# A DLRM tower: ten tables looked up by matmul instead of nine, two late tables for three chunks instead of two, and the whole order of the later stages rewritten

## The reference

```python
e = jnp.stack([tbl_0[ids[:, 0]], ..., tbl_26[ids[:, 26]]], axis=1)      # (512, 27, 128)
interactions = jnp.einsum('bfd,bgd->bfg', e, e)
x = interactions.reshape(B, F * F)[:, TRIL_IDX]                          # 351 pairs, i > j
h = jnp.concatenate([bottom, x, bottom], axis=1)                         # (512, 607)
h = jnp.maximum(h @ W_top1 + b_top1, 0.0)                                # 512 wide
h = jnp.maximum(h @ W_top2 + b_top2, 0.0)                                # 256 wide
y = h @ W_top3
```

## Time and profile before

| | |
|---|---|
| median of 3 runs | 121.84 us (120.61 to 122.99) |
| the profiled execution's own time | 119.64 us |
| its span | 117.5 us |
| busy: PE, DVE, ACT, POOL | 92.8, 74.8, 63.7, 72.8 us |
| gathers | 68, of 1.05 us on average |
| mean DMA rate | 121 GB/s |

### The profile page before, as it was taken

How to read it: one execution, slowest core, us unless ns; L and a number is a source line. 1 busy time by engine, 2 the same in 40 slices (tenths; PEclk the granted TensorE clock), 3 DMA queues, 4 the chain that set the end, 5 groups by cost and what they waited for, 6 DMA issues and landing times.

```text
span 117.5 us, 3583 instructions
## 1 busy us (share of the span) xinstructions
PE 92.8 (79%) x1464; PEld 77.8 (66%) x1464; DVE 74.8 (64%) x230; ACT 63.7 (54%) x150; POOL 72.8 (62%) x75
## 2 busy tenths in 40 slices
PE   6608999999899999794458399955899838992992
PEld 6503788878688788583357299843798718980990
DVE  5418899999999999864994062164154656793001
ACT  7525698997996985563162162361165506990010
POOL 2777777777777787777777777677677620001000
PEclk9999999999999999999999967999999999999689
DMA  3749999999999767793112212113122220000000
GB/s 39 164 132 261 252 248 237 242 244 247 230 242 234 179 165 214 290 300 92 46 45 76 62 50 67 50 50 86 49 59 59 58 58 6 0 6 21 0 0 1
DMA packets 7347, 14.28 MB, mean 121 GB/s; under 512 B 2149, under 2 KB 4485, under 8 KB 7332
## 3 DMA queue, kind: packets, MB, share of 16 engines
q1 hardware_dynamic: 5104, 9.58, 32.8%
q0 software_dynamic: 2208, 4.47, 14.5%
q10 hardware_dynamic: 20, 0.01, 0.1%
HBM read 13.81 MB, written 0.00 MB: 118 GB/s over the span
## 4 chain that ended last, share of the span: by engine, by line
POOL 59%; issue 18%; PE 10%; DMA 6%; DVE 3%; ACTq 1%; DVEq 0%
POOL rows L309 59%; PE pH L587 5%; DMA rows<-in_tbl,ids_sb 3%; DVE Z L342 3%; PE pT L587 2%; PE pG L613 2%; DMA ids_sb<-in_ids 2%; DMA Z<-Z 1%; PE pF L538 1%; ACTq L247 1%; PE pT L527 1%; DVE prod L484 0%; DVE ET L321 0%; DVEq L129 0%
## 5 line engine op out<-in xcount | busy, mean ns | idle before, releaser
L309 POOL DMA_INDIRECT rows<-in_tbl,ids_sb x68 | 71.6, 1054 | 21.6 <-issue 20.4
L465 DVE TENSOR_SCALAR hot<-ids_b,row_f 125x512 fp32r<-125x512 int16 (+1 forms) x75 | 31.8, 452 | 1.7 <-DMA ids_b<-in_ids_t 1.7
L342 DVE COPY Z<-pG 26x96 f32<-26x96 f32 (+1 forms) x80 | 19.5, 244 | 19.5 <-PE pG L613 18.5
L342 ACT COPY Z<-pG 26x96 f32<-26x96 f32 (+1 forms) x80 | 18.7, 234 | 16.3 <-PE pG L613 15.4
L563 PE MATMUL pG<-hot,high 125*128 125x512 f32 x72 | 22.0, 422 | 4.7 <-ACT high L352 4.2
L563 PE MATMUL pG<-hot,low 125*128 125x512 f32 x72 | 20.2, 404 | 0.0
L462 DVE TENSOR_TENSOR low<-tbl,high 125x256 fp32r<-125x256 f32 x44 | 18.2, 414 | 3.1 <-ACT high L352 3.1
L563 PEld LDWEIGHTS pG<-hot,high 125*128 125x128 f32 x72 | 13.6, 196 | 9.3 <-ACT high L352 4.5
L613 PE MATMUL pG<-ET 128*26 128x26 f32 x1024 | 13.5, 194 | 7.1 <-issue 4.6
L613 PEld LDWEIGHTS pG<-ET 128*26 128x26 f32 x1024 | 11.2, 104 | 10.1 <-issue 7.9
L563 PEld LDWEIGHTS pG<-hot,low 125*128 125x128 f32 x72 | 14.1, 196 | 3.1
(11 more groups left out here) (39 smaller groups left out, 57.6 us busy)
## 6 DMA issues: line engine op xcount, KB each, us to landing
tbl<-in_tbl SPq DMA_DIRECT2D x11, 448.0 KB
ids_b<-in_ids_t SPq DMA_DIRECT2D x9, 128.0 KB, 5.2
rows<-in_tbl,ids_sb POOLq DMA_INDIRECT x68, 5.0
W1Z<-in_w_tiles SPq DMA_DIRECT2D x1, 768.0 KB
tbl<-in_tbl SPq DMA_DIRECT2D x11, 52.0 KB
W1A_B<-in_w_ab SPq DMA_DIRECT2D x1, 512.0 KB, 3.8
W2S<-in_W_top SPq DMA_DIRECT2D x1, 512.0 KB
botT<-in_bottom_t SPq DMA_DIRECT2D x1, 256.0 KB, 4.0
```

The lines of the kernel that those rows point to most:

```text
L309: pool.indirect_dma_start(out=rows[:, c % 2, slot[f], :], out_offset=None, in_=tables[f][:, :], in_offset=bass.IndirectOffsetOnAxis(ap=ids ...
L342: last = engine_copy(to[:, :, STAGE - n:STAGE, :, s, :], of)
L465: nc.vector.tensor_scalar(hot[0:TP, n % 2, k, columns(n)], ids_b[0:TP, n % TABLE_RING, columns(n)], row_f[0:TP, k:k + 1], None, ALU.is_equ ...
```

## The change

- `N_ONE_HOT` 9 to 10: one more table is looked up for all samples. `LATE_FROM` 2 to 1: the two late tables are looked up for samples 128 to 511, 384 columns instead of 256. All twelve 1000-row tables are now looked up. Gathers: 17 + 15 + 15 + 15 = 62. Chunks 1 and 2 have seven runs instead of six, the last chunk eight instead of seven.
- In `look_up` PE takes all 8 blocks of `high`, then all 8 of `low`; DVE makes all its `hot` blocks and then the four `low` parts, where they alternated.
- The first table is loaded and rounded in two halves, and the second table's loads no longer wait for the first ids. SP's loads of weights don't wait for the last table or for `W1A_B`. ACT copies the previous lookup before it makes one-hot blocks.
- 72 warm-up matmuls instead of 34.
- DVE prepares **both** late tables ahead of the first Z move; before, the second came after the first unit of chunk 0.
- Both gram units of a chunk stand back to back. The first dense layer of a chunk follows the next chunk's grams, and in the last step chunk 2's first and second layers also stand ahead of chunk 3's last transposes; chunk 3's four gram units stand together.

```diff
-N_ONE_HOT = 9
+N_ONE_HOT = 10
-LATE_FROM = 2
-WARM_UP = (20, 14)
+LATE_FROM = 1
+WARM_UP = 72
...
-                elif n:
-                    sp.wait_ge(ids_b_in[n - 1], 16)
...
-            sp.wait_ge(tbl_in[N_ALL - 1], 32)
...
-            sp.wait_ge(w1ab_in, 16)
...
             prepare(N_ONE_HOT)
+            prepare(N_ONE_HOT + 1)
             for c in range(LAST):
-                first, *others = units_of(c)
-                move_gram(nc.vector.tensor_copy, dve, first, 0, z_dve)
-                runs_of(c + 1, 0, BETWEEN[c])
+                for k in units_of(c):
+                    move_gram(nc.vector.tensor_copy, dve, k, 0, z_dve)
+                runs_of(c + 1, 0, 2)
                 if c == 0:
-                    prepare(N_ONE_HOT + 1)
                     dve.wait_ge(w1ab_in, 16)
                     nc.vector.tensor_tensor(W1AB[:, :], W1A_B[:, 0, :], W1A_B[:, 1, :], ALU.add).then_inc(w1ab_done, 1)
-                for k in others:
-                    move_gram(nc.vector.tensor_copy, dve, k, 0, z_dve)
-                runs_of(c + 1, BETWEEN[c], RUNS[c + 1] - LATE_RUNS[c + 1])
+                runs_of(c + 1, 2, 4)
                 if c:
                     dense3(c - 1)
-                runs_of(c + 1, RUNS[c + 1] - LATE_RUNS[c + 1], RUNS[c + 1])
+                if c + 1 == LAST:
+                    dense3(c)
+                runs_of(c + 1, 4, RUNS[c + 1])
...
+                for k in units_of(c):
+                    gram_unit(k)
+                next_run()
+                next_run()
                 if c == 0:
                     look_up(N_ONE_HOT)
+                    next_run()
+                    look_up(N_ONE_HOT + 1)
+                    next_run()
+                    dense_layer1_bottom(c)
                 else:
+                    dense_layer1_pairs(c - 1)
+                    next_run()
+                    dense_layer2(c - 1)
+                if c + 1 < LAST:
+                    while len(waiting):
+                        next_run()
+                    if c:
+                        dense_layer1_bottom(c)
+                else:
                     dense_layer1_bottom(c)
+                    dense_layer1_pairs(c)
+                    next_run()
+                    dense_layer2(c)
+                    while len(waiting):
+                        next_run()
```

More of the change, by code:

```diff
@@ L200, in dlrm_tower_kernel @@
         z_dve = sem("z_dve")
-        packed = sem("packed")
+        packed = [sem(f"packed_{c}") for c in range(CHUNKS)]
         packed_pool = sem("packed_pool")
@@ L532, in dense_layer2 @@
                     pe.wait_ge(lookup_moved, N_ALL)
+                    pe.wait_ge(weights_in, 3 * 16)
                 if 0 < c < LAST:
@@ L543, in _ @@
             pe.wait_ge(warm_done, 1)
-            for x in range(sum(WARM_UP)):
+            for x in range(WARM_UP):
                 nc.tensor.matmul(pF[:, 0:P], warm[:, :], warm[:, :], start=True, stop=True)
@@ L550, in look_up @@
                     pe.wait_ge(lookup_moved, n)
-                half = TABLE_K // 2
-                first, second = range(half), range(half, TABLE_K)
-                for x, (part, blocks) in enumerate(((high, first), (low, first), (high, second), (low, second))):
-                    if x == 0:
-                        pe.wait_ge(high_done, n + 1)
-                    for k in blocks:
+                for part in (high, low):
+                    for k in range(TABLE_K):
+                        if part is high and k % (TABLE_K // 2) == 0:
+                            pe.wait_ge(high_done, n + 1 + (n > 0 or k > 0))
                         if part is high and k < TABLE_K - act_blocks[n]:
@@ L564, in look_up @@
                                                 hot[0:TP, n % 2, k, columns(n)],
-                                                start=x == 0 and k == 0, stop=x == 3 and k == TABLE_K - 1)
+                                                start=part is high and k == 0, stop=part is low and k == TABLE_K - 1)
                 last.then_inc(looked_up, 1)
@@ L633, in _, with next_run @@
                     pe.wait_ge(mover(i), moved_until(c, i))
-                waiting = list(range(RUNS[c + 1] - LATE_RUNS[c + 1]))
-                def next_run(until):
-                    if waiting and waiting[0] < until:
-                        transpose_run(c + 1, waiting.pop(0))
-                first, *others = units_of(c)
-                gram_unit(first)
-                next_run(BETWEEN[c])
+                waiting = list(range(RUNS[c + 1]))
+                def next_run():
+                    transpose_run(c + 1, waiting.pop(0))
@@ L657, in _ @@
-                while waiting and waiting[0] < BETWEEN[c]:
-                    next_run(BETWEEN[c])
-                for k in others:
-                    gram_unit(k)
-                next_run(len(RUNS) * P)
-                if c == 0:
-                    dense_layer1_bottom(c)
-                    look_up(N_ONE_HOT + 1)
-                next_run(len(RUNS) * P)
-                if c:
-                    dense_layer2(c - 1)
-                if c + 1 == LAST:
-                    dense_layer1_bottom(c)
@@ L687, in _ @@
             pe.wait_ge(h2_done, LAST)
-            nc.tensor.matmul(pF[:, :], ones[0:1, :], b2_sb[0:1, :], start=True, stop=False)
+            nc.tensor.matmul(pF[:, 0:N2], ones[0:1, :], b2_sb[0:1, :], start=True, stop=False)
             wait_packed(LAST)
```

105 lines of the change are left out of this document (45 added, 60 removed).

## The result

| | before | after |
|---|---|---|
| median | 121.22 us (120.29 to 122.99) | 131.67 us (129.8 to 131.97) |
| profiled execution, its span | 119.64, 117.5 us | 131.37, 129.6 us |
| gathers: number, mean, last one starts | 68, 1.05 us, 93.92 | 62, 1.28 us, 99.92 |

The change makes the kernel slower: ratio 1.080, 95% interval 1.057 to 1.103. Medians are of all executions; a ratio with an interval compares only the undisturbed ones of both kernels. The forecast was 123.4 us with a range up to 126.8, most likely a difference too small to tell, so it was wrong.

What follows compares the result with a forecast made beforehand. The prediction took POOL's gathers to bound the kernel before, then summed DVE's and PE's serial steps to 116.9 us, plus 1.4 for a stop and 0.8 for low clock: span 119.1, time 123.4 us, range 120.4 to 126.8.

Steps and rivals of the forecast that it cites:

- What the change removes: Six gathers on POOL: the last starts at 86.4 instead of 93.9 us, worth 7.5 us if gathers stayed the bound.
- The front: Work up to DVE's first Z move: moved from 51.0 to 55.2 us by table work; PE's added work costs nothing.
- the forecast's 55.2: Start of DVE's first Z move in us, summed as 49.5 - 2.7 + 3.8 + 0.5 + 4.1.
- From Z moves to chunk 1's grams: From DVE's 55.2 us through Z moves, copies, second late lookup and transposes; chunk 1's grams start at 66.0 us.
- Stops: PE halts inside gram units with "issue" as only cause, 1.43 and 1.36 us before; one of 1.4 us counted.
- the stops add up: Slower rival: second late lookup at low clock (2 us) plus two PE stops (2 x 1.4); time 126.0 us; chance 35%.
- The low clock: PE at 1.2 GHz after mostly standing, possibly in the second late lookup; 0.8 us counted.
- From chunk 2's to chunk 3's grams: Grams, Z moves, packs, chunk 2's dense layers and last transposes, all in series: 19.2 us, from 78.1 to 97.3.
- The tail: From chunk 3's first grams to the end of the span: 20.2 - 0.6 = 19.6 us.
- The gathers stay the bound: Faster rival: POOL's gathers still bind, so fewer of them shorten the span to 109.4, time 113.7 us; chance 3%.
- Sum: Whole span: 116.9 + 1.4 for a stop + 0.8 for low clock = 119.1 us, against 117.5 before.
- up to 96 us everything but POOL has slack: Before the last rows land at 96.3 us, only POOL's queue of gathers binds; the other engines' slack can be spent.

Runs made afterwards that it cites:

- alternate_2: The changed kernel with DVE again alternating one-hot blocks and `low` parts, nothing else undone: median 128.3 us, ratio to the kernel before 1.046 (1.038 to 1.053).

## Why the prediction was wrong

**The step that failed** is in "What the change removes" and "The front": the last gather "starts at 48.9 + 30 x 1.25 = 86.4", "up to 1 us more" while DVE prepares tables longer, and so chunk 0's grams on PE cost nothing. The prediction saw the slow pace of the front (1.49 us a step) and put it down to DVE's work, but took its amount as the thing that counts. What counts is how long DVE's one-hot blocks run without a break: the same blocks in rows of six and seven make steps of up to 4.5 us. Gather 32 was 13.0 us late against before, and the last one 13.5 against the forecast. By the trace this moved DVE's first Z move by 5.4 us. The experiments give it 3.4% (1.080 to 1.046, 4.1 us of 121) in the new order, where undoing it brings the waits for roundings back, and 4.0% in the old. That DVE makes all its blocks and then the `low` parts stood in the prediction only as a gain of 2.7 us. The rule of the Trainium skill named above spoke against that edit and was not weighed.

**The front otherwise.** With the gathers free, alternate_2's Z moves start at 59.0. DVE's first block is 1.5 us later there than before (7.49 against 5.94), and it waits 2.6 us in all for roundings and for PE (1.03, 0.60, 0.53 and 0.46), which the forecast's 55.2 had at nothing: 59.3. The sum of DVE's parts held to 0.3 us. PE's grams of chunk 0, forecast for 49.5 to 51, started at 54.15 there and at 58.18 in the changed kernel; that cost nothing, as DVE was later still. The late blocks at 384 columns, taken as 0.34 us, measured 0.34 (eight in 2.72), and the `low` parts 0.34. In the changed kernel the first ids landed 1.1 us later than before. The loads now issued ahead of time are the likely cause: in all six traces with SP's dropped waits that block starts at 6.53 to 7.51 us, in all nine with the waits at 5.59 to 6.45, and restoring them in the changed kernel gave 6.45. What the delay costs in time no run at the pace of the result tells, but the forecast's "nothing" for the dropped waits was too little.

**From Z moves to chunk 1's grams**: 10.8 forecast, 11.2 measured. Right.

**Stops.** The mechanism was right, even to the 250 instructions, and the term was mis-sized. I counted one of 1.4 us; on the path stood 1.82, 1.41 and 1.75, 5.0 us in all. "Of the eight stretches of 128 gram matmuls there, five had none" was the wrong evidence: single stretches of 128 cross at most two borders with rest ahead of them, and the change puts two stretches together. The rival "the stops add up" (35%) had named just this; its 2.8 us was too small too.

**The low clock.** 0.8 forecast; one set of 24 pair matmuls took 3.79 us at 95.19 instead of 2.84, 1.0 us, at a granted clock of 0.73, after the two stops at 89.91 and 93.46. Right in size. It was not where I looked for it, in the second late lookup (67.31 to 70.19, 2.9 us at a granted clock of 1.00, where 2.8 was forecast at full clock).

**From chunk 2's to chunk 3's grams**: 19.2 forecast; 22.6 measured, of which 3.2 are stops and 1.0 is clock, so 18.4 of work. The tail, 19.6 against 19.8, was right.

**"The gathers stay the bound"** got 3%. In its own words (faster) it didn't happen. But the gathers did bind, in the front, and not as a gain given up but as a loss; no rival had that.

**Sum.** 119.1 forecast. Held gathers 5.4, ids 1.1, stops beyond the one counted 3.6, and 0.4 from small terms that partly cancel make 129.6, the span that was measured. The 0.4 is what was left over, not a forecast.

**What the lost gain was.** Even alternate_2, without held gathers, is 4.6% slower. The chain of before said "POOL 59%", and the 7.5 us that six gathers take were read rightly, but "up to 96 us everything but POOL has slack" was too much: the second-longest path, PE and DVE, was right behind. The tenth table alone, in the old order, costs 1.4% with four gathers fewer; the new order costs some 4% at 256 columns. The parts don't add up to one sum, since each edit also moves the stops to other places.

## What to carry to other kernels

Look at how long an engine runs one kind of operation without a break, not at its sum: where GpSimd issues gathers, alternate DVE's `tensor_scalar` blocks with other operations, as the kernel before did, instead of a long row of each, and compare the longest gather before and after. Short matmuls with a weight load each (14 ns for two instructions) eat instructions faster than they are fetched: in stretches of 256 such matmuls each stop cost 0.9 to 2.4 us, and of the stretches of 128 in the kernel before five of eight had none, so keep them apart with longer matmuls, and count where the stops fall before and after. To judge an order, run both orders with the same work in them. A chain that is 59% one queue says what a shorter queue can bring only together with the slack of the next path; try one step of it before giving work to the other engines.

## What the runs showed of the hardware

A gather that takes 0.95 us alone took up to 4.60 us beside rows of six to seven one-hot blocks (2.4 to 2.9 us) with `low` parts ahead of them, and ended 0.20 us behind the row. PE's fetch stops stay at fixed counts of its instruction stream, to within three matmuls, when the program is shifted by 126 instructions. And one occasion isn't another: on the first, the kernel before took 159.8 us instead of 121 to 122, and 121.65 later on a chip of the same number, so what made it slower is open. A 10-table kernel in the old order was level with before there (159.05) but 4.4% behind later, by the medians, so a comparison holds for the occasion on which it was made.
